# Attention A's `k` and `pos` operands: 48 of their 96 rows read from memory, the other 48 copied on chip

## What is computed

```python
def _relative_shift(x):
    b, h, s, _ = x.shape
    x = jnp.pad(x, ((0, 0), (0, 0), (0, 0), (1, 0)))
    x = x.reshape(b, h, s + 1, s)
    return x[:, :, 1:, :].reshape(b, h, s, s)
...
q = heads(x @ Wq + bq)
k = heads(x @ Wk + bk)
val = heads(x @ Wv + bv)
pos = _sinusoid_pos_emb(S, D) @ Wp + bp
pos = pos.reshape(S, H, P).transpose(1, 0, 2)
content_score = jnp.einsum('bhsp,bhtp->bhst', q + u, k)
pos_score = jnp.einsum('bhsp,htp->bhst', q + v, pos)
pos_score = _relative_shift(pos_score)
score = (content_score + pos_score) / jnp.sqrt(jnp.float32(P))
weights = jax.nn.softmax(score, axis=-1)
out = jnp.einsum('bhst,bhtp->bhsp', weights, val)
```

## Time and profile before

| | us |
|---|---|
| median of 3 runs | 9964.28 |
| lowest and highest run | 9959.06 to 9972.98 |
| the profiled execution | 9955.88 |
| its span, first to last instruction | 9954.1 |

### The profile page before, as it was taken

The page is one execution under the profiler, slowest core; times in us unless marked ns, Lnnn a source line. Parts: engine busy times, 40 slices in busy tenths (PEclk is TensorE's granted clock), DMA queues, the critical chain, the costliest instruction groups (busy, mean ns, idle before and its releaser), DMA issues. The chain is left out here.

```text
span 9954.1 us, 256407 instructions
## 1 busy us (share of the span) xinstructions
PE 8957.4 (90%) x91488; PEld 5840.8 (59%) x91488; DVE 6024.0 (61%) x12530; ACT 5585.1 (56%) x10811; POOL 2778.8 (28%) x2894
## 2 busy tenths in 40 slices
PE   6988999899899998989989999998998898999899
PEld 4666666445566666644556666664555666666455
DVE  4666664664466666467456666646745666663673
ACT  4666664454466666445456666634545666663454
POOL 3333332100333333210033333321003333332101
PEclk8999999899999999989989999998998999999899
DMA  8999994110799999321079999922108999992210
GB/s 320 399 390 392 405 399 164 68 33 26 286 404 395 397 395 401 146 71 34 24 305 403 398 397 406 402 111 73 34 24 335 397 401 392 404 402 89 74 35 24
DMA packets 440126, 2552.03 MB, mean 256 GB/s; under 512 B 60016, under 2 KB 90224, under 8 KB 176368
## 3 DMA queue, kind: packets, MB, share of 16 engines
q1 hardware_dynamic: 438768, 2534.40, 64.7%
HBM read 1284.53 MB, written 1248.85 MB: 255 GB/s over the span
## 5 line engine op out<-in xcount | busy, mean ns | idle before, releaser
L825 POOL TENSOR_SCALAR z<-z,nmax 128x1024 f32<-128x1024 f32 x2048 | 2270.3, 1120 | 3655.7 <-DVE nmax L774 3655.7
L764 DVE CUSTOM_DVE_ANT_0 z<-sc,z 128x1024 f32<-128x1024 f32 x2048 | 2496.0, 1219 | 1190.6 <-DMA z<-rel_rows 1179.9
L721 ACT ACTIVATE rel<-rg 128x512 f32<-128x512 f32 x3072 | 1721.8, 596 | 1594.4 <-PE rg L598 880.2
L726 ACT ACTIVATE pT<-rg 128x512 f32<-128x512 f32 x4096 | 2226.9, 595 | 519.9 <-PE rg L631 519.3
L631 PE MATMUL rg<-ident,z 128*128 128x128 f32 x16384 | 2186.8, 277 | 3.7 <-ACT pT L726 3.2
L631 PEld LDWEIGHTS rg<-ident,z 128*128 128x128 f32 x16384 | 1785.8, 143 | 504.1 <-issue 361.2
L1075 ACT ACTIVATE pT<-rg 128x512 f32<-128x512 f32 (+3 forms) x2560 | 1226.1, 531 | 829.7 <-PE rg L1007 498.7
L1091 DVE TENSOR_REDUCE mx_b<-sc 128x1 f32<-128x1024 f32 (+7 forms) x1024 | 1004.0, 991 | 471.3 <-PE sc L989 235.5
L652 PE MATMUL op<-pT,xnT 128*32 128x128 f32 x32768 | 1118.7, 278 | 4.8 <-DVE rel L803 4.0
L797 DVE COPY rel<-rg 128x512 f32<-128x512 f32 x1024 | 708.3, 692 | 454.6 <-PE rg L602 422.5
L984 PE MATMUL sc<-z 96*128 96x512 bf16 (+3 forms) x2560 | 765.6, 370 | 149.5 <-DMA z<-k_parts 74.2
(11 more groups left out here) (115 smaller groups left out, 8871.8 us busy)
## 6 DMA issues: line engine op xcount, KB each, us to landing
rel_rows<-rel SPq DMA_DIRECT2D x1024, 1088.0 KB, 9.1
z<-rel_rows SPq DMA_DIRECT2D x1024, 1024.0 KB, 9.6
v_heads<-rel SPq DMA_DIRECT2D x8, 4096.0 KB, 14.2
xnT<-v_heads SPq DMA_DIRECT2D x128, 256.0 KB, 4.3
qu_parts<-z SPq DMA_DIRECT2D x36, 512.0 KB, 4.4
pos_s<-pos_parts SPq DMA_DIRECT2D x64, 192.0 KB, 9.4
qv_parts<-z SPq DMA_DIRECT2D x24, 512.0 KB, 6.7
k_parts<-z SPq DMA_DIRECT2D x24, 512.0 KB, 5.6
```

The costliest lines, as they stand in the source:

```text
L721: e.activation(rel[:, r % RING, c * CH:(c + 1) * CH], rg[:, R_BANK[c], :], ACT.Copy).then_inc(r_copied[c], 1)
L726: e.activation(pT[:, t % 2, q * CH:(q + 1) * CH], rg[:, T_BANK[q], :], ACT.Exp, scale=SCALE).then_inc(p_ready[q], 1)
L764: e.tensor_tensor_reduce(out=zs, in0=scf[:, 2 * half * CH:2 * (half + 1) * CH], in1=zs, scale=1.0, scalar=-3.0e38, op0=ALU.add, op1=ALU.ma ...
L825: e.tensor_scalar(zs, zs, 1.0, nmax[:, n % 2:n % 2 + 1], ALU.mult, ALU.add).then_inc(AA[done], 1)
```

## The change

`load_moving` is used no more in attention A. `load_once` reads each of a group's 16 memory rows once, into the first of its rows, with the semaphore `pos_once` or `k_once`. `repeat_rows` waits for the landing of all three groups of a set and issues three DMAs from SBUF to SBUF, 16 rows each: two for the first group, one for the second. PE's waits are as before, since the three copies take the count of the three loads in `QK_INC`. The standing operands' loads stay.

```diff
         QK_INC = 16 * 2 * len(GROUP)
+        ONCE = 16 * len(GROUP)
...
             if kind == "A":
                 for hd in range(NB):
                     for i in range(len(GROUP)):
-                        load_moving(e, pos_s[hd], pos_d, hd, i, qv_loaded[hd])
+                        load_once(e, pos_s[hd], pos_d, hd, i, pos_once[hd])
...
                 for i in range(len(GROUP)):
                     load_still(e, qv_s[0], qv_d, 0, i, qv_loaded[0])
+                for hd in range(NB):
+                    v = e.snap(b * (nh // NB * ONCE) + ONCE)
+                    repeat_rows(e, pos_s[hd], pos_once[hd], v, qv_loaded[hd])
...
+        def load_once(e, k, k_src, h, i, done):
+
+            first, last, reps = GROUP[i]
+            e.dma_start(k[first:last:2 * reps, :], k_src[i:i + 1, bass.ds(h, 1), :, 0:S]
+                        .rearrange("r a d s -> (r a d) s")).then_inc(done, 16)
+
+        def repeat_rows(e, k, landed, count, done):
+
+            e.wait_ge(landed, count)
+            settle(e)
+            for first, last, reps in GROUP:
+                for r in range(1, reps):
+                    e.dma_start(k[first + 2 * r:last:2 * reps, :], k[first:last:2 * reps, :]).then_inc(done, 16)
...
-            load_pair(e, qu_s[0], k_s[0], qu_d, k_d, 0, range(len(GROUP)), AA["qk_loaded0"])
+            for i in range(len(GROUP)):
+                load_still(e, qu_s[0], qu_d, 0, i, AA["qk_loaded0"])
+                load_once(e, k_s[0], k_d, 0, i, k_once[0])
...
-            def second_head(s):
+            def second_head(base, s):
...
+                elif s == len(GROUP) + 1 - R_LEAD:
+                    repeat_rows(e, k_s[0], k_once[0], e.snap(base.once + ONCE), AA["qk_loaded0"])
...
-                    load_pair(e, qu_s[nxt], k_s[nxt], qu_d, k_d, e.snap(p * HB + (hd + 1)), ((at - 1) // 2,),
-                              AA[f"qk_loaded{nxt}"])
+                    load_still(e, qu_s[nxt], qu_d, e.snap(p * HB + (hd + 1)), (at - 1) // 2, AA[f"qk_loaded{nxt}"])
+                    load_once(e, k_s[nxt], k_d, e.snap(p * HB + (hd + 1)), (at - 1) // 2, k_once[nxt])
+                if at == 7 and not (final and hd + 1 >= HB):
+                    repeat_rows(e, k_s[nxt], k_once[nxt], e.snap(base.once + ((hd + 1) // NB + 1) * ONCE),
+                                AA[f"qk_loaded{nxt}"])
...
-                    load_pair(e, qv_s[hd % NB], pos_s[hd % NB], qv_d, pos_d, e.snap(p * HB + (hd + 2)), ((at - 8) // 2,),
-                              qv_loaded[hd % NB])
+                    load_still(e, qv_s[hd % NB], qv_d, e.snap(p * HB + (hd + 2)), (at - 8) // 2, qv_loaded[hd % NB])
+                    load_once(e, pos_s[hd % NB], pos_d, e.snap(p * HB + (hd + 2)), (at - 8) // 2, pos_once[hd % NB])
+                if at == 14 and not (final and hd + 2 >= HB):
+                    repeat_rows(e, pos_s[hd % NB], pos_once[hd % NB],
+                                e.snap(base.once + ((hd + 2) // NB + 1) * ONCE), qv_loaded[hd % NB])
```

More of the change, by code:

```diff
@@ L92 @@
 ROWS = dict(bv=0, bo=1, Bbv=2, Bbo=3, b2=4)
-Counts = namedtuple("Counts", "tiles fours moves pairs values")
+Counts = namedtuple("Counts", "tiles fours moves pairs values once")
 Marks = namedtuple("Marks", "heads blocks pieces groups pairs values rows steps")
@@ L259, in program @@
         qv_loaded = [sem("qv_loaded0"), sem("qv_loaded1")]
+        pos_once = [sem(f"pos_once{k}") for k in range(NB)]
+        k_once = [sem(f"k_once{k}") for k in range(NB)]
         tail_full = sem("tail_full")
@@ L567, in counts @@
                 return Counts(*(e.snap(b * (nh // HB * per) + p * per)
-                                for per in (G, G // OB, 16 * G // RING, HB // NB * QK_INC, HB // NB * 16)))
+                                for per in (G, G // OB, 16 * G // RING, HB // NB * QK_INC, HB // NB * 16, HB // NB * ONCE)))
             with e.Fori(0, 1) as p:
@@ L926, in step @@
                 else:
-                    second_head(s)
+                    second_head(base, s)
             in_order(e, b, step)
```

## The result

The kernel with the change takes 10041.51 us (median of 4 runs, 10026.56 to 10048.23) beside 9966.31 us of the kernel before on the same chip: a ratio of 1.0074, with a 95% interval of 1.0062 to 1.0087. It is **75 us slower** (62 to 87), where 21 us were predicted; 10041.51 lies 6.5 us above the range.

The account below looks back on a forecast made before the run. It took DMA transfers as the limit in attention A. Start loss 34 us less steady gain 13 us gave 21 us on 9964.3: 9985 us, range 9932 to 10035.

Parts of the forecast that it names:

- What bounds the kernel: Attention A: transfers are the limit, DMA share 1.00 at 398 GB/s; delays cost only as far as the engines run dry.
- my sign for starved reads: Steady part of attention A: a DMA share below 0.99 outside the loop turns would show late reads starving the queue.
- What the change removes: Sets loaded inside the full queue: 25 MB fewer memory reads, 0.11 us gained a set, 13 us over 116 sets.
- the estimate of 0.17 us: `k` and `pos` sets: gain a set by the port rule alone, only the first group's rows spreading better over ports.
- The other rule that I weighed: Skill's rule: about 358 GB/s between memory and SBUF, 436 only within SBUF; weighed for the memory-slow rival, chance 0.17.
- What it adds in the steady part: Three more DMAs a set on SP delay the next `z` read 0 to 2.5 us, covered by the queue: no cost.
- Its cover is the queue: Steady part: the previous read lands 9.7 us after issue, so about 4.5 us of queued work hides a late read.
- late reads starve the queue: Steady part: loads landing later than 9.6 us run engines dry 0.4 us at each `z` read: 10031 us, chance 0.12.
- The start of a pass: Four times a pass start: meeting 2.6 us later plus first head's `k` copies 6 us, 34 us lost (22 to 58).
- the start is covered: Pass start: the queue's 14 us hold out, only the meeting costs, 4 x 3.2 = 13 us: 9964 us, chance 0.24.
- (a): Pass start: SP issues six `pos` copies before meeting the other engines, 2.6 us lost in full each pass.
- The rates that I named as signs: Steady part: 399 to 401 GB/s at share 1.00 if the forecast holds, 404 or more if memory was slow.

Follow-up runs that it names:

- copies_first: steady_only with a step's loads, waits and copies issued between SP's read of `z` and its write: 9935.4 us, 0.9973 of the kernel before.
- read_late: The kernel before, with SP counting a semaphore up 50 or 42 times between write and next read in steps 7 and 14, no DMA added: 10055.1 us, 1.0100.
- reload_first: reload_wait with a step's loads, waits and repeated reads issued between SP's read of `z` and its write: 9934.4 us, 0.9978 of the kernel before.
- split_first: The kernel before, each broadcast `k` or `pos` load cut into one to three 16-row DMAs, loads issued between read and write: 9993.3 us, 1.0030.
- steady_only: The changed kernel with the start of a pass as before it, copies only in the steady part: 10020.8 us, 1.0057 of the kernel before.
- read_later: read_late with 80 and 72 semaphore counts, holding the read back further: 10165.8 us, 1.0210 of the kernel before.
- loads_first: The kernel before, with a step's loads issued between SP's read of `z` and its write: 9970.8 us, 1.0008 of the kernel before.
- reload_wait: steady_only with the repeated rows read from memory again, same places, waits and three DMAs: 9977.0 us, 1.0018 of the kernel before.
- start_only: The changed kernel with copies only at the start of a pass, broadcast loads in the steady part: 10009.1 us, 1.0044 of the kernel before.
- copies_moved: steady_only with only the waits and copies moved behind the next read, ahead of its write (steps 8 and 15): 9964.0 us, 1.0001 of the kernel before.
- spread12: The kernel before, with all sets issued as twelve 16-row DMAs a pair, rows six partitions apart, attention A and B: 10172.7 us, 1.0212.

## Why the prediction was wrong

**What bounds the kernel.** Right: the kernels that slow the stage clearly show a lower rate (396, 393, 385 GB/s), the one that speeds it a higher one (400 in copies_first). But I read the share for more than it says: I counted a loss only where "the DMA engines run dry", and looked for it in the share. The share is 1.00 in the earlier trace rows, in the changed kernel and in read_late. Even inside the trough of read_late (step 7, 4 to 10 us behind the write) the mean share over the same heads is 0.92 to 1.00, where the rate has fallen from 420 to between 320 and 370 GB/s. So my sign for starved reads, a share below 0.99, stayed away although reads were late; only the GB/s show it.

**What the change removes: 0.11 us a set.** The sign holds where the reads are not held back: copies_first gains 25 us over 116 sets, 0.21 us each. My reason was wrong. With reload_first equal, what is gained is neither memory traffic nor the freedom from the source's partitions. split_first and reload_first issue the same six DMAs of 16 rows from memory; the one has them all with the loads (+28), the other has three of them behind the landing (-26). Even without the 15 us that split_first loses outside attention A's steps, some 40 remain between the two, which points to the spreading of a set over more steps; no run changed that alone. That the estimate of 0.17 us from the Trainium skill's port rule lies near the measured 0.21 proves nothing for it: no run here tests its mechanism. The other rule that I weighed (the Trainium skill, "SBUF — State Buffer", "Summary: rules for kernel authors", a higher rate within SBUF than from memory) would have set copies ahead of loads from memory. The trace does not agree: behind the read they are alike (9935.4 against 9934.4), ahead of it the copies are 44 us behind.

**What it adds in the steady part: nothing on the path.** This is the step that failed: the copies in the steady part cost 48 us (the changed kernel's trace) to 59 (steady_only) net of what they gain, where the path had nothing and the net was -13. Its lateness was right: the next read came 1.1 us late in step 14 and 2.1 us in step 7 (means of steady_only), where I had 0 to 2.5 (the terms as I gave them, 1.3 + 3.6 - 2.0, allow 2.9). The wait for the landing, about which I worried, held up nothing: the first copy is issued 0.2 us behind the write in the mean, 0.3 at most. The lateness comes from the three issues, 2.6 to 2.8 us together. What was wrong is the sentence "Its cover is the queue: the read issued one step before lands 9.7 us after its issue (...), so about 4.5 us of work is ahead of it". The landing was as I had it: the read of the step before lands 6.2 to 6.4 us behind the write's issue. But the landing is the end of its last packet, and the rate does not come back at a late read's issue either (issued at 406.32 in read_later, back at 411.5). The table above has the true cover: the rate holds for 4 to 5 us behind the write's issue, and a read that is issued 2 us behind it just makes that. There was no slack of 4.5 us but less than 1.1, since at 0.6 next to nothing is lost and at 1.1 the trough is there. It fits that loads_first, which brings the reads of steps 2 and 9 from 2.6 and 2.4 us back to 2.0, gained nothing. Taken over all their 116 places, read_late and read_later lose 0.83 and 1.8 us a place for a mean lateness of 1.4 and 3.2 us, more than half of every us. That is no fixed price: for 1.6 us steady_only loses 0.7 us a place against copies_first, and for 1.5 us reload_wait 0.35 against reload_first.

**The rival "late reads starve the queue"** came nearest the mechanism and gave 10031. It wanted loads that land later than 9.6 us, which they did not, and a delay of 4.5 us, with 0.4 us at each place; steady_only's whole loss is 0.5 us a set, and 0.7 us against copies_first. A chance of 0.12 was too low, as it hung on the same cover.

**The start of a pass: 34 us.** Right in kind and about in size. The meeting is 2.6 us later, as worked out; content comes 14.5 us later after it (28.8 us behind the first row matmul, 14.3 before), where 13.5 stood; the first score 10.5, where 9.5 stood. PE's new wait for `k_sb<-k_sb` is 60.7 us in four passes, 15.2 each. start_only costs 47 us (27 to 61), the start inside the changed kernel about 34 in its profiled execution. The 4 x 3.2 us of the rival "the start is covered" do not follow from (a), which has 2.6; the start was not covered, so nothing hangs on it.

**The sum.** 34 - 13 = 21 became 75. The range ended at the starved rival with the start as forecast, 10035; with the steady part at 59 and the start as forecast, 9964 + 34 + 59 = 10057, the time was outside of it already. The rates that I named as signs (399 to 401 if right) did tell: 396.

**What stays open.** Three small DMAs ahead of the read hold it back by 1.2 and 0.6 us and cost no more than behind it (19 and 25 us); by read_late's price 60 us more were due. Whether the small DMAs fill the gap that the late read leaves, or read_late's counts cost something besides (its program is longer: 4.88 MB of instructions fetched by one queue instead of 4.62), was not settled. Nor is it shown what the queue lacks in the trough: that it begins when the read of the step before is running out and only the write is left is my reading of the times, not a run's result. Open too is why lateness costs 84 us with copies in the gap, 41 with loads from memory and 96 with nothing. copies_moved is 24 us behind copies_first, which moves the loads too, while moving the loads alone gains nothing; that pair I can't explain.

## What to carry to other kernels

On one queue of long transfers in turn, put extra issues where they do not stand ahead of the transfer whose issue is already the tightest: here the same copies cost 59 us ahead of the read, nothing behind it (copies_moved), and gain 25 where the loads are moved as well. Measure cover in GB/s after the last issue, not by the landing of the transfer ahead and not by the busy share, which stayed at 1.00. And test a change of source (memory or SBUF) against its twin in the same place before giving the source the credit, and in more than one place: here the twins are equal behind the read and 44 us apart ahead of it.

## What the runs showed of the hardware

- A read of 1 MB issued 2.1 us late took the queue from 420 GB/s down to between 304 and 370 for 5 us (step 7 of read_late and steady_only), in a stage whose DMA share still reads 1.00.
- Small DMAs are not free in a full queue: three of 512 bytes, 116 times, cost 25 us with all else on time. The moving operands' bytes in 16-row DMAs of 64 KB cost 28 us with the reads on time (split_first, attention B's loads included), and all sets in such DMAs 205 us with the reads late as well (spread12, windows, first pass, 388 GB/s):

```profile
180.00:1550.00 1370.00, 1226.31 (x13864) 873.83 (x13863) 895.97 (x1972) 861.12 (x1624) 515.54 (x465) 0.96 0.99 388
```

- A 64 KB copy within SBUF was no cheaper than the same 64 KB from memory: its rows landed in 6.9 us, where the load of 64 KB took 8.6 (the changed kernel's DMA view of 180 to 1550 us, issues, KB, median us to landing), and yet the time is the same behind the read (copies_first, reload_first) and 44 us longer ahead of it (steady_only, reload_wait).

```profile
pos_s<-pos_parts SPq DMA_DIRECT2D x42, 64.0 KB, 8.6
pos_s<-pos_s SPq DMA_DIRECT2D x42, 64.0 KB, 6.9
```
